# Graph-network kernel, second layer: scatter-adds in turn to three tables of node sums instead of four

## The reference

```python
h = jnp.maximum(_layernorm(x, axis=-1), 0.0)
x_j = h[dst]                                              # [edges, 16]
m = silu(einsum('ei,ej,ijh->eh', x_j, edge_attr_8, W_msg_tp) * norm_msg_tp)
m = m @ W_msg_lin * norm_lin
agg = segment_sum(m, src, num_segments=12500)             # sums by src: not sorted
u = silu(einsum('ni,nh,ihk->nk', h, agg, W_upd_tp) * norm_upd_tp)
x = x + h + u @ W_upd_lin * norm_lin
```

## Time and profile before

| | |
|---|---|
| median of 3 runs | 8827.98 us (8803.6 to 8840.02) |
| profiled execution, its own time | 8860.82 us |
| its span | 8859.1 us |
| TensorE busy | 7393.8 us, 83% of the span |
| VectorE busy | 6501.9 us, 73% |
| GpSimd (POOL) busy | 5659.4 us, 64% |
| ScalarE busy | 4441.1 us, 50% |
| 1616 scatter-adds, L1503 | 2545.4 us, 1575 ns mean |

### The profile page before, as it was taken

One profiled execution on the slowest core, in us unless ns is written; L12 is line 12 of the kernel. 1 busy time (PEld: TensorE's weight loads), 2 busy tenths in 40 slices (PEclk: granted clock), 3 DMA queues, 4 the chain that ended last, 5 costly groups with the idle time before them and its releaser, 6 DMA issues. The chain is left out here.

```text
span 8859.1 us, 189093 instructions
## 1 busy us (share of the span) xinstructions
PE 7393.8 (83%) x52097; PEld 6326.6 (71%) x52097; DVE 6501.9 (73%) x16875; ACT 4441.1 (50%) x8258; POOL 5659.4 (64%) x4883
## 2 busy tenths in 40 slices
PE   5777777777777777777777778599999999999997
PEld 4555665656665566665555656499999999999996
DVE  5555665656665566665565656799999999999997
ACT  2333333333333333333333333478888877778874
POOL 4555555555555555555555556288888888878884
PEclk8888888888888888888888888799999999999999
DMA  2000000000000000000000001444444455554443
GB/s 45 14 14 14 15 15 15 15 14 15 15 15 14 14 15 15 15 15 14 14 14 14 15 14 29 94 73 75 74 74 75 73 73 73 73 72 73 75 73 55
DMA packets 702285, 335.45 MB, mean 38 GB/s; under 512 B 422862, under 2 KB 645928, under 8 KB 702256
## 3 DMA queue, kind: packets, MB, share of 16 engines
q0 software_dynamic: 336128, 66.50, 12.4%
q1 hardware_dynamic: 364946, 265.19, 11.9%
q10 hardware_dynamic: 1182, 3.44, 0.1%
HBM read 301.49 MB, written 33.15 MB: 38 GB/s over the span
## 5 line engine op out<-in xcount | busy, mean ns | idle before, releaser
L703 POOL DMA_INDIRECT xg<-gather_rows,idx x3232 | 3082.3, 954 | 2385.2 <-PE ps_w L813 1140.4
L813 PE MATMUL ps_w<-W2s,hT 128*128 128x256 f32 x12928 | 3432.4, 417 | 446.2 <-issue 418.2
L813 PEld LDWEIGHTS ps_w<-W2s,hT 128*128 128x128 f32 x12928 | 2707.9, 210 | 1131.7 <-issue 687.0
L1503 POOL DMA_INDIRECT sums<-total,row x1616 | 2545.4, 1575 | 564.9 <-issue 440.8
L1468 PE MATMUL ps_wide<-hot_col,placed 128*128 128x392 f32 x12928 | 2439.0, 346 | 15.8 <-issue 9.6
L742 ACT ACTIVATE hT<-ps_h,b1c 128x512 f32<-128x512 f32 x1616 | 1018.6, 681 | 2721.4 <-remote 2163.2
L1468 PEld LDWEIGHTS ps_wide<-hot_col,placed 128*128 128x128 f32 x12928 | 2317.7, 196 | 29.8 <-issue 22.9
L877 DVE TENSOR_TENSOR prod<-ps_w,xg 128x512 f32<-128x512 f32 x1616 | 1095.9, 690 | 1118.0 <-remote 560.8
L1401 ACT ACTIVATE square<-iota_col,minus_col 128x784 bf16<-128x784 int16 x1212 | 1060.5, 937 | 88.5 <-issue 66.1
L1306 DVE SCALAR_TENSOR_TENSOR placed<-ps_r,src_r,halves 128x512 fp32r<-128x512 f32 x1616 | 1096.9, 740 | 0.1
L884 DVE TENSOR_REDUCE msg<-prod 128x32 f32<-128x512 f32 x1616 | 1059.1, 676 | 0.0
(11 more groups left out here) (187 smaller groups left out, 4954.4 us busy)
## 6 DMA issues: line engine op xcount, KB each, us to landing
dst_row<-dst_rows SPq DMA_DIRECT2D x404, 256.0 KB
xg<-gather_rows,idx POOLq DMA_INDIRECT x3232
src_row<-src_rows SPq DMA_DIRECT2D x404, 128.0 KB
q_win<-q_rows SPq DMA_DIRECT2D x404, 96.0 KB
ea<-in_edge_attr SPq DMA_DIRECT2D x404, 64.0 KB
sums<-total,row POOLq DMA_INDIRECT x1616
e<-in_edge_attr SPq DMA_DIRECT2D x404, 32.0 KB
q_rows<-Q SPq DMA_DIRECT2D x13, 768.0 KB, 3.5
```

The lines of the kernel that those rows point to most:

```text
L703: pool.indirect_dma_start(xg[r][:, t, :], None, k.rows, bass.IndirectOffsetOnAxis(ap=idx[r][:, t:t + 1], axis=0)).then_inc(xg_in[r][t], 16)
L813: last = pe.matmul(bank[:, w, :, :].rearrange("p i o -> p (i o)"), hT[half][:, j, col:col + P], k.W2[:, j, :], start=(j == 0), stop=(j == 1))
L1503: pool.indirect_dma_start(k.sums[t], bass.IndirectOffsetOnAxis(ap=row[r][:, t:t + 1], axis=0), total[r][:, t, :], None, compute_op=ALU.add ...
```

## The change

`SUMS = 3` tables take the scatter-adds. The tuple `TURN` says for each of the 16 scatters of a lap (4 groups of 4 tiles) which table it goes to; table 0 has six of them and the others five each. A scatter waits until all former scatters to its table have landed; `adds` works out the semaphore's count from the lap. ScalarE's wait before `total` uses the same counts, for which its body needs the number of the lap; `each_ring` gets a parameter for more unrolled laps ahead, and ScalarE uses two. The wide sums go to `k.sums[3]`. `clear_tables` clears three tables, and `finish` loads and adds four.

```diff
-TABLES = TP + 1
+SUMS = 3
+TURN = (0, 1, 2, 0, 1, 2, 0, 1, 2, 0, 1, 2, 0, 1, 0, 2)
+TABLES = SUMS + 1
...
-def each_ring(engine, count, body, ring=4):
-    for c in range(ring):
-        body(c, c, 0)
+def each_ring(engine, count, body, ring=4, laps=1):
+    for c in range(laps * ring):
+        body(c, c % ring, c // ring)
     assert count % ring == 0
-    with engine.Fori(0, (count - 2 * ring) // ring) as i:
+    with engine.Fori(0, count // ring - laps - 1) as i:
         for u in range(ring):
-            body(i * ring + (ring + u), u, i + 1)
+            body(i * ring + (laps * ring + u), u, i + laps)
...
-    for t in range(TP):
+    for t in range(SUMS):
         flat = k.sums[t][0:S.N, :].rearrange("a b -> (a b)").rearrange("(p f) -> p f", p=125)
...
-    added = [sem(f"sum_added{t}") for t in range(TP)]
+    added = [sem(f"sum_added{j}") for j in range(SUMS)]
+    assert len(TURN) == RING * TP
+
+    def adds(j, lap, r, t):
+
+        return 16 * TURN.count(j) * lap + 16 * TURN[:TP * r + t].count(j)
...
-                def total_out(g, r):
+                def total_out(g, r, lap):
 
                     a.wait_ge(q["rowf_ready"], g + 1)
-                    for t in range(TP):
-                        need(a, added[t], 16 * (g - RING + 1))
+                    for j in range(SUMS):
+                        need(a, added[j], adds(j, lap - 1, r, TP))
...
-                each_ring(a, G, body, RING)
+                each_ring(a, G, body, RING, 2)
...
                     for t in range(TP):
-                        need(pool, added[t], 16 * g)
+                        j = TURN[TP * r + t]
+                        need(pool, added[j], adds(j, lap, r, t))
 
                         pool.sem_inc(q["scatters_begun"], 1)
                         pool.indirect_dma_start(
-                            k.sums[t], bass.IndirectOffsetOnAxis(ap=row[r][:, t:t + 1], axis=0),
-                            total[r][:, t, :], None, compute_op=ALU.add).then_inc(added[t], 16)
+                            k.sums[j], bass.IndirectOffsetOnAxis(ap=row[r][:, t:t + 1], axis=0),
+                            total[r][:, t, :], None, compute_op=ALU.add).then_inc(added[j], 16)
```

More of the change, by code:

```diff
@@ L539, in clear_tables @@
         engine.dma_start(k.sums[t][S.N:, :], k.zeros[:, 0:D]).then_inc(zeroed, 16)
-    engine.wait_ge(zeroed, 16 * TP * (len(per) + 1))
+    engine.wait_ge(zeroed, 16 * SUMS * (len(per) + 1))
 class Norm:
@@ L1220, in _ @@
                 each(sp, G, body, head=4, tail=2)
-                table = k.sums[TP][0:HI * S.LO, :].rearrange("(c r) f -> c (r f)", r=HI)
+                table = k.sums[SUMS][0:HI * S.LO, :].rearrange("(c r) f -> c (r f)", r=HI)
                 full, (i, n) = len(turns) - 1, turns[-1]
@@ L1418, in body @@
                     if not isinstance(g, int) or g >= 1:
-                        total_out(g - 1, (r - 1) % RING)
+                        total_out(g - 1, (r - 1) % RING, lap if r else lap - 1)
                         rows_out(g - 1, (r - 1) % RING)
                     columns(g, s)
-                each_ring(a, G, body, RING)
-                total_out(G - 1, RING - 1)
+                each_ring(a, G, body, RING, 2)
+                total_out(G - 1, RING - 1, G // RING - 1)
                 rows_out(G - 1, RING - 1)
@@ L1499, in scatter @@
                     for t in range(TP):
-                        need(pool, added[t], 16 * g)
+                        j = TURN[TP * r + t]
+                        need(pool, added[j], adds(j, lap, r, t))
                         pool.sem_inc(q["scatters_begun"], 1)
                         pool.indirect_dma_start(
-                            k.sums[t], bass.IndirectOffsetOnAxis(ap=row[r][:, t:t + 1], axis=0),
-                            total[r][:, t, :], None, compute_op=ALU.add).then_inc(added[t], 16)
+                            k.sums[j], bass.IndirectOffsetOnAxis(ap=row[r][:, t:t + 1], axis=0),
+                            total[r][:, t, :], None, compute_op=ALU.add).then_inc(added[j], 16)
                 each_ring(pool, G, scatter, RING)
-                for t in range(TP):
-                    pool.wait_ge(added[t], 16 * G)
+                for j in range(SUMS):
+                    pool.wait_ge(added[j], adds(j, G // RING, 0, 0))
                 pool.dma_reset()
```

## The result

The kernel with three tables takes 8935.7 us, the kernel before 8845.3 us in the runs made beside it (14 runs each); the ratio is 1.0087, with a 95% interval of 1.005 to 1.0124, so about 77 us slower (44 to 110). The ratio is that of the means, taken over the 13 runs of each kernel that lie within 1.5% of its fastest; the two medians lie 90 us apart. The profiled execution of after has a time of 8980.9 us, a span of 8979.0 us and a mean granted clock of 0.908.

A forecast was written before the change was run, and what follows sets the result against it. TensorE sets the pace, but POOL has no reserve beside it and would bind: loop +82.6 us, +76.8 after 5.8 of cover, last stage -1, sum +76, so 8904 us; range 8812 to 8965.

The forecast's parts named there:

- The bound: Second layer's loop: TensorE sets the pace at 30.1 us a lap, and POOL, also at 30.1, has no reserve.
- The 0.5 us of stretching: POOL's longer scatters, 0.5 us a lap: all the slack POOL has, if they go when it is late.
- The lap of 31.15 us: POOL's lap in the second layer's loop: 29.6 + 0.5 + 1.1 us, over TensorE's 30.1.
- the 1.1 us of waits: POOL's added waits for earlier scatters, 1.1 us a lap in all, bounds 0.2 and 1.7.
- price of 0.7 us for a pair at a random phase: A scatter waiting for the one two before costs 0.7 us on average over landing phases, 1.4 a lap.
- The waits at distance three: Scatters waiting for the one three before (5.54 us) add 0 to 0.3 us a lap.
- The delay after a landing: On POOL, 0.86 us from a wait's end to the scatter's start, plus 0.2 us for the semaphore.
- The ring: The four buffers of `total` leave some 18 us of delay free, used up after some 20 laps.
- The end: At the loop's end POOL's 5.8 us of cover leave +76.8 us; the last stage gives -1 us.
- The signs: If right: two late scatters a lap, 7.7 to 7.9 us a group, TensorE under 295 of 300 us, longer ScalarE waits.
- TensorE as the bound: Rival: POOL's stretching goes when late, its lap stays at 30.1 us, time 8822 us, not slower; chance 0.28.
- late binding: Rival: POOL binds late in the loop, a lap of 30.4 to 30.8 us, 8828 to 8868 us; chance 0.12.

The follow-up runs named there:

- e1: The change's code with four tables in turn (0, 1, 2, 3), against the kernel before: 7416.8 against 7415.3 us, ratio 1.0001.
- e4: The change with four tables, two scatters a lap at distance two and the rest at four or more: ratio 1.009 to the kernel before.
- e7: The change with the source rows placed 312 rows further on in DRAM: ratio 1.0055 to the kernel before.
- e8: Four tables at distance four with the change's code, source rows 312 rows further on in DRAM: ratio 0.9991 to the kernel before.
- e5: The change with the destination-row load cut from 128 to 16 partitions, fifth group to third from last: ratio 1.0013 to the kernel before.
- e6: Four tables by turn, destination-row load cut from 128 to 16 partitions, fifth group to third from last: ratio 0.9979 to the kernel before.
- third batch: Follow-up kernels run beside the kernel before on a chip like the first, where the kernel before takes 8893 us.
- e2: The change with two tables in turn, every scatter waiting for the one two before: 7948.0 us, ratio 1.0716 to the kernel before.

## Why the prediction came out right

**The bound.** Right: POOL has next to no reserve beside TensorE. e1, with no added wait, runs laps of 30.0 us, and the change's excess above that shows in the lap: 0.6 us outside for a lap of 30.6, 2.6 inside for 32.8. The 0.5 us of stretching did not go when POOL was late (1576 ns a scatter, 1575 before), so it was no slack. But the reserve was not nil: in before POOL waited some 60 us of its loop for ScalarE's rows (107.7 less the 47 ahead of the first scatter), in after 5. The new waits took the place of these before they made the lap longer.

**The lap of 31.15 us.** The loop is 3146.2 us long, where 101 laps of 31.15 us less 1.85 give 3144.3: +84.5 us against the +82.6 of the sum. But the 1.1 us of waits are right only as a mean, and what makes them is otherwise spread than I had it: outside groups 200 to 300 it is 0.6 us a lap, inside 2.6. My price of 0.7 us for a pair at a random phase was over twice too high outside (0.26 us a pair) and near inside (0.79). Outside, I had the late phases too frequent: 0.3 of them, where 17% of all landings take over 3.5 us. With 1.13 us of delay, all landings together would make it 0.45 us. The rest is that the pairs meet few of the late ones (5% over 3.5 us), as the prediction thought POOL would. The waits at distance three, "0 to 0.3 us a lap", are 0.33 over the loop, just over their bound, but 1.04 inside. Two errors of the terms cancelled, and that the sum came within 2 us is luck: I had no term for a stretch with slower loads, though the rows of the three slow slices stood in the profile; I took their loss, 11 us at most, for noise of TensorE's and did not ask what landed late in them.

**The delay after a landing.** 0.86 us from a wait's end, plus 0.2 for the semaphore, is 1.06; measured 1.13. A quiet landing is 2.6 us, and 2.6 + 1.13 = 3.73 against a spacing of 3.70: at distance two a quiet landing costs next to nothing, and any other costs in full. At distance three the limit is 5.54 - 1.13 = 4.4 us, which under 1% of the landings pass outside, 19% inside. The 1.13 is of distance two; behind the late landings that hold up a scatter at distance three the delay is longer, 1.4 to 1.5 us at the median.

The Trainium skill (Perfetto Trace Analysis, DMA Instruction — SWDGE (GPSIMD)) says that the profile ends such an instruction when its descriptors are made, not when the data has moved. The traces agree: a row of 1.54 us, packets done 2.6 us and later after its start. The Trainium skill's fit of 2.0 us for a small transfer (DMA: Bandwidth & Descriptors, Anatomy of one DMA — SWDGE (gpsimd) path), by which no pair would wait, doesn't hold for these scatter-adds: in e4 the pairs alone cost 0.9%.

**The ring.** `total`'s four buffers take the first 18 us, I said, for some 20 laps. Measured: the lag of a group's first scatter behind its `total` rises from 2.7 us to 20 at group 200, the 50th lap, is 22 to 24 until group 300 and 21 to 22 after that, some 19 us above the start; it comes later than said, since the lap outside is shorter. The ring spares nothing in the end: the lag is still there at the last scatter, which ends the stage. From there ScalarE and TensorE wait as named (31.4 us at `sum_rows` in 7300 to 8200).

**The end.** The cover of 5.8 us was used up as said: the stage starts 6.0 us behind the last scatter instead of 12.0. The last stage is shorter by 0.9 us, for -1 predicted; one table less gives nothing more, since `bd_upd`, which `aT` waits behind, still starts 11.4 us into the stage, before 11.75.

**The sum.** 84.5 - 6.0 - 0.9 = 77.6 us, against +76; and the ratio's 77 us (44 to 110). The two profiled executions lie 120 us apart, because the first scatter of after comes 42 us later: layer 0 is the same code in both but for one table's clear, and the start of the first scatter moves by that much between kernels and executions (5678, 5708 and 5747 us in the third batch's three).

**The other chips.** There the same change cost more, 1.47% or 109 us (98 to 120), and its loop is 121 us longer than e1's. Its own loop is alike on the two chips (3146 and 3157 us); what differs is the loop with four tables, 3036 us there for 3062. POOL's rows say where: in e1 it waits only 9 us of its loop for ScalarE's rows, where before had 60 us whose place the new waits could take. So the forecast lap was good on both chips, and the +76 us hold for a kernel before that loses some time of its own. Why its loop is 26 us slower on the first chip isn't known.

**The signs.** ScalarE's long waits, the late scatters (169 in 101 laps) and a last scatter near 8830 (8836, less the 42 us of the later start) were there; "TensorE under 295 of 300 us" held in three slices only, and 7.7 to 7.9 us a group was the mean of about 7.65 outside and 8.2 inside.

**The rivals.** TensorE as the bound is out, with waits of 0.6 us a lap even outside the stretch. Without that stretch the change would cost 0.55% (e7), and "late binding" would have been the case that came.

**Still open.** Why the source rows are slow to read in groups 197 to 307. e7 and e8 tie it to the place in DRAM, e5 and e6 to the load beside it, whose own packets are slower there too; which of the tensors' addresses meet wasn't tried, and the shift moved all tensors placed behind `src_rows` too.

## What to carry to other kernels

Before a buffer or table is taken from a chain of asynchronous scatters, set the spacing of its uses against the whole round trip: landing plus the time from landing to the next start, here 2.6 + 1.1 us in the quiet and, for the latest hundredth beside loads, 4.9 us and 1.1 to 1.5 more, and not the 1.54 us that the engine's row shows. Share them out evenly: two pairs two apart in sixteen cost more than all the distances of three. Where a stretch of the loop is slower than the rest in the profile of before, find out what is slow in it first, as it is there that a thinner reserve gives way.

## What the runs showed of the hardware

The same broadcast load of 128 KB, in packets of 1024 bytes, took about 50 ns a packet from most rows of a DRAM tensor and 72 to 144 ns from about rows 197 to 307, in the kernel before and on each of the three chips of the experiments; in the kernel before the packets of SyncE's queue took 32.3% instead of 24.6% of the engines' time. It was gone when the rows lay 312 rows further on (49 ns), and the packets took about 65 ns throughout when the destination load was cut to an eighth. To the kernel with four tables this mattered little: with quick packets (e8) it took 0.1% less, by the interval at most 0.2%. The scatters landed 0.3 us later in the mean in the slow rows (3.3 for 3.0, after), and three tables had no room for that.

A scatter-add of 128 rows of 64 bytes landed 2.6 us (the earliest tenth) to 4.9 us (the latest hundredth) after its POOL row began, though the row ends after 1.54 us. A scatter that waited for it at distance two began 1.13 us after the landing (median of 106, after; 1.15 us in e2).
